# A selective scan in a four-layer decoder: the products with B move from TensorE to GpSimd

## The reference

```python
def _mamba_forward(x, ln_g, ln_b, W_in, conv_w, conv_b, W_x, W_dt, dt_bias, A_log, D, W_out):
    L = x.shape[1]
    xn = _layer_norm(x, ln_g, ln_b)
    xz = jnp.einsum('ble,de->bld', xn, W_in)
    u, z = (xz[..., :DIN], xz[..., DIN:])
    up = jnp.pad(u, ((0, 0), (DCONV - 1, 0), (0, 0)))
    uc = sum((conv_w[:, k] * up[:, k:k + L, :] for k in range(DCONV))) + conv_b
    u = jax.nn.silu(uc)
    dbc = jnp.einsum('bld,rd->blr', u, W_x)
    dt_in = dbc[..., :DTR]
    Bm = dbc[..., DTR:DTR + DSTATE]
    Cm = dbc[..., DTR + DSTATE:]
    dt = jax.nn.softplus(jnp.einsum('blr,dr->bld', dt_in, W_dt) + dt_bias)
    dA = jnp.exp(dt[..., None] * -jnp.exp(A_log))
    dBu = dt[..., None] * Bm[:, :, None, :] * u[..., None]

    def step(h, e):
        da, dbu, c = e
        h = da * h + dbu
        y = jnp.einsum('bdn,bn->bd', h, c)
        return (h, y)
    ...
    _, ys = jax.lax.scan(step, h0, elems)
    y = (jnp.moveaxis(ys, 0, 1) + u * D) * jax.nn.silu(z)
    return x + jnp.einsum('bld,ed->ble', y, W_out)
```

## Time and profile before

| quantity | value |
|---|---|
| median of 3 runs | 1628.07 us (1625.56 to 1632.83) |
| profiled execution | 1626.36 us |
| its span | 1624.5 us |
| mean granted clock of PE | 0.961 of full speed |
| busy, whole span | PE 1413.6, DVE 953.5, ACT 685.6, POOL 348.1 us |
| first and last start of a scan | 554.0 and 754.2 us |
| 554.0 to 600.8 us | PE busy 44.8, DVE 26.4, ACT 23.5, POOL 13.0 us |

### The profile page before, as it was taken

The page is one execution under the profiler, slowest core; times in us unless marked ns, Lnnn a source line. Parts: engine busy times, 40 slices in busy tenths (PEclk is TensorE's granted clock), DMA queues, the critical chain, the costliest instruction groups (busy, mean ns, idle before and its releaser), DMA issues.

```text
span 1624.5 us, 25636 instructions
## 1 busy us (share of the span) xinstructions
PE 1413.6 (87%) x9708; PEld 918.2 (57%) x9708; DVE 953.5 (59%) x2240; ACT 685.6 (42%) x1932; POOL 348.1 (21%) x293
## 2 busy tenths in 40 slices
PE   7999776888787999998887638989998999989997
PEld 4666543555555566665554425555566666656664
DVE  2556567666654455566767786655675455653334
ACT  4555324565554544342454203632234555422222
POOL 1333004433431232131500034200100333410000
PEclk9999989999998999999998979999999999999999
DMA  9000000000000400000000000000000000000000
GB/s 375 1 1 1 1 1 1 1 1 1 1 1 14 196 1 1 0 1 1 1 2 1 0 1 1 2 1 0 0 2 2 1 1 1 1 1 1 0 0 13
DMA packets 4225, 25.72 MB, mean 16 GB/s; under 512 B 1168, under 2 KB 3216, under 8 KB 3472
## 3 DMA queue, kind: packets, MB, share of 16 engines
q1 hardware_dynamic: 4112, 24.19, 3.7%
HBM read 23.67 MB, written 0.52 MB: 15 GB/s over the span
## 4 chain that ended last, share of the span: by engine, by line
PE 72%; DVE 15%; ACT 6%; issue 4%; POOL 1%; DMA 1%; DVEq 0%; SPq 0%; ACTq 0%; POOLq 0%
PE PS L1071 6%; PE PS L641 5%; PE PS L1056 4%; PE PS L1057 4%; PE PS L325 4%; PE PS L1912 4%; PE PS L357 3%; PE PS L1890 3%; PE PS L337 3%; PE PS L707 3%; PE PS L1903 2%; PE PS L298 2%; PE PS L306 2%; PE PS L366 2%; PE PS L319 2%
## 5 line engine op out<-in xcount | busy, mean ns | idle before, releaser
L549 POOL TENSOR_TENSOR arena<-arena,small 128x768 f32<-128x768 f32 (+1 forms) x64 | 107.8, 1684 | 225.7 <-DVE small L492 116.8
L877 DVE TENSOR_REDUCE arena<-PS 128x2 f32<-128x512 f32 (+1 forms) x192 | 108.8, 609 | 53.5 <-PE PS L635 52.4
L804 ACT ACTIVATE arena<-PS 128x512 f32<-128x512 f32 (+1 forms) x192 | 92.2, 532 | 107.2 <-PE PS L641 107.2
L2104 DVE TENSOR_TENSOR_SCAN arena<-arena,PS 128x512 f32<-128x512 f32 x64 | 78.1, 1220 | 81.3 <-PE PS L1890 70.3
L1160 DVE TENSOR_TENSOR arena<-arena,PS 128x512 f32<-128x512 f32 x82 | 56.4, 688 | 117.1 <-ACT arena L1093 117.0
L1093 ACT ACTIVATE arena<-PS 128x512 f32<-128x512 f32 x82 | 49.0, 597 | 167.9 <-PE PS L1057 167.9
L429 ACT ACTIVATE arena<-PS,small 128x256 f32<-128x256 f32 (+1 forms) x256 | 110.8, 453 | 0.0
L641 PE MATMUL PS<-arena 32*128 32x256 f32 (+1 forms) x768 | 97.7, 371 | 13.8 <-DVE arena L877 9.5
L635 PE MATMUL PS<-arena 32*128 32x256 f32 (+1 forms) x768 | 94.7, 372 | 2.2 <-DVE arena L877 1.6
L500 DVE COPY arena<-PS 128x768 f32<-128x768 f32 (+1 forms) x64 | 69.5, 1086 | 34.6 <-PE PS L337 34.6
L641 PEld LDWEIGHTS PS<-arena 32*128 32x128 f32 x768 | 64.0, 185 | 42.3 <-ACT arena L804 30.4
...
## 6 DMA issues: line engine op xcount, KB each, us to landing
...
w_rest<-in_rest SPq DMA_DIRECT2D x1, 6493.5 KB, 38.3
...
```

The costliest lines, as they stand in the source:

```text
L549: g.tensor_tensor(p, p, ri, ALU.mult).then_inc(self.pn_done.sem, 1)
L804: a.activation(self.PT[:, q % 8, :], PS[:, 3 + q % 3, 0:2 * n], ACT.Exp).then_inc(self.e_done.sem, 1)
L877: v.tensor_reduce(dst, src, AX.X, ALU.max, negate=True).then_inc(self.mx_done.sem, 1)
```

## The change

The products dt*u*B are no longer matmuls. For each step PE spreads the row of B over the partitions like that of C (`spread_b`), up to five steps ahead, into bank 5; ACT copies it to one of four SBUF buffers (`b_copy`); GpSimd multiplies it with dt*u (`product`) into one of four SBUF buffers `dB`; and the scan reads decays and products, both from SBUF. The transposes, the diagonals and the copy `turned` are gone.

Both spreads are now bf16 matmuls. So that no precision is lost, B and C are computed three times, on partitions 0, 32 and 64, and `parts` on GpSimd turns them into three bf16 parts (a value rounded to bf16, what is left rounded, and what is left then), which one matmul over 96 partitions adds up. The row of C has one bank (4) in place of two, the sum over the states one (6) in place of two; B's spread and the output projection share bank 5. The next batch's `inputs` are cut into four pieces of two matmuls (n = 0 to 3) and `gates` (n = 4); ACT's silus, selections and logarithms come one step later each; `gate` comes at n = 1 and `finish` at n = 4. The decays keep four buffers, at another place of the arena.

```diff
@@ Mamba.__init__
-        self.dc_done, self.dc_ev, self.bt_ev = s("dc_done", B, 1), s("dc_ev", B, 1), s("bt_ev", B, 1)
+        self.dc_done, self.dc_ev = s("dc_done", B, 1), s("dc_ev", B, 1)
+        self.part_step = s("part_step", 7 * B, 1)
-        self.tr_done, self.tr_ev = s("tr_done", B, 1), s("tr_ev", B, 1)
-        self.diag_ready = s("diag_ready", G // 4, 1)
-        self.da_ready, self.db_done, self.c_done = s("da_ready", G, 1), s("db_done", G, 1), s("c_done", G, 1)
+        self.b_done, self.bs_ready, self.db_ready = s("b_done", G, 1), s("bs_ready", G, 1), s("db_ready", G, 1)
+        self.da_ready, self.c_done = s("da_ready", G, 1), s("c_done", G, 1)
...
-        self.CB, self.BT = t(4108, 2, 256), t(4620, 2, 32)
-        self.ab, self.rl, self.lw, self.ex = t(4684, 512), t(5196, 512), t(5708, 512), t(6220, 512)
-        self.dt, self.dtu = t(6732, 2, 512), t(7756, 512)
-        self.dtuT = t(8268, 2, 2, 256)
-        self.diag = t(9292, 24, P)
-        self.dA = t(12364, 4, 512)
-        self.h, self.hC = t(14412, 2, 512), t(15436, 3, 512)
-        self.y = t(16972, 512)
+        self.DBC, self.BC = t(4108, 2, 256), t(4620, 256).bitcast(BF16).rearrange("p (b s) -> p b s", b=2)
+        self.rest = t(4876, 256)
+        self.ab, self.rl, self.lw, self.ex = t(5132, 512), t(5644, 512), t(6156, 512), t(6668, 512)
+        self.dt, self.dtu = t(7180, 2, 512), t(8204, 512)
+        self.bs, self.dB = t(8716, 4, 256), t(9740, 4, 512)
+        self.h, self.hC = t(11788, 2, 512), t(12812, 3, 512)
+        self.y = t(14348, 512)
         self.r = t(0, 512)
+        self.dA = t(14860, 4, 512)
@@ tensor
...
+            for k in taps:
+                ins = pe.matmul(PS[:, self.bank(b, part), part * 256:part * 256 + 256],
+                                self.WK[:, k, part * P:(part + 1) * P], self.XNT[:, b, k:k + 256],
+                                start=(k == 0), stop=(k == 3), skip_group_check=True)
+            if taps[-1] == 3:
+                ins.then_inc(self.uz_done.sem, 1)
...
-            for t in range(2):
-                for j in range(2):
-                    ins = pe.matmul(PS[:, 0, 256 + t * 16:272 + t * 16], u[:, j * 256 + t * P:j * 256 + t * P + P],
-                                    self.wB[:, j, :], start=(j == 0), stop=(j == 1), skip_group_check=True)
...
-        def turn(b):
-            pe.wait_ge(self.chain_step.sem, self.chain_step.at(0, 5 * b + 5))
-            pe.wait_ge(self.bt_ev.sem, self.bt_ev.at(0, b + 1))
-            for t in range(2):
-                for j in range(2):
-                    ins = pe.transpose(PS[:, 0, t * 256 + j * P:t * 256 + j * P + P],
-                                       self.dtu[:, j * 256 + t * P:j * 256 + t * P + P], c.ident)
-            ins.then_inc(self.tr_done.sem, 1)
-
-        def drive(g):
+        def spread_b(g):
             b, n = divmod(g, self.N)
             if n == 0:
-                pe.wait_ge(self.tr_ev.sem, self.tr_ev.at(0, b + 1))
-            if n % 4 == 0:
-                pe.wait_ge(self.diag_ready.sem, self.diag_ready.at(0, g // 4 + 1))
+                pe.wait_ge(self.part_step.sem, self.part_step.at(0, 7 * b + 7))
             if g == 0:
-                pe.wait_ge(self.xn_ev.sem, self.xn_ev.at(0, 1))
-            elif g == 1:
                 pe.wait_ge(self.xn_ev.sem, self.xn_ev.at(0, 2))
             else:
-                pe.wait_ge(self.sc_ready.sem, self.sc_ready.at(0, g - 1))
-            for t in range(2):
-                for j in range(2):
-                    ins = pe.matmul(PS[:, 2 + g % 2, j * 256 + t * P:j * 256 + t * P + P],
-                                    self.dtuT[:, b % 2, t, j * P:(j + 1) * P], self.diag[:, g % 12 * 2 + t, :],
-                                    start=True, stop=True, skip_group_check=True)
-            ins.then_inc(self.db_done.sem, 1)
-
-        def spread(g):
+                pe.wait_ge(self.bs_ready.sem, self.bs_ready.at(0, g))
+            if b and n == 9:
+                pe.wait_ge(self.z_ready.sem, self.z_ready.at(b - 1, 1))
+            pe.matmul(PS[:, 5, 0:256], self.onehot[0:96, n:n + 1].to_broadcast([96, P]),
+                      self.BC[0:96, b % 2, :], start=True, stop=True).then_inc(self.b_done.sem, 1)
...
+
+        def spread_c(g):
             b, n = divmod(g, self.N)
+            if n == 0:
+                pe.wait_ge(self.part_step.sem, self.part_step.at(0, 7 * b + 7))
             if g == 0:
                 pe.wait_ge(self.xn_ev.sem, self.xn_ev.at(0, 3))
-            if n == 0:
-                pe.wait_ge(self.dc_ev.sem, self.dc_ev.at(0, b + 1))
-            if g >= 2:
-                pe.wait_ge(self.hc_ready.sem, self.hc_ready.at(0, g - 1))
-            pe.matmul(PS[:, 4 + g % 2, 0:256], self.onehot[32:48, n:n + 1].to_broadcast([16, P]),
-                      self.CB[32:48, b % 2, :], start=True, stop=True).then_inc(self.c_done.sem, 1)
+            else:
+                pe.wait_ge(self.hc_ready.sem, self.hc_ready.at(0, g))
+            pe.matmul(PS[:, 4, 0:256], self.onehot[0:96, 16 + n:17 + n].to_broadcast([96, P]),
+                      self.BC[0:96, b % 2, :], start=True, stop=True).then_inc(self.c_done.sem, 1)
...
+            if b and n == 0:
+                pe.wait_ge(self.y_ready.sem, self.y_ready.at(0, b))
...
+            g = min(self.N * (b + 1) + 9, self.G)
+            pe.wait_ge(self.bs_ready.sem, self.bs_ready.at(0, g))
...
-        keep_warm(c, pe, 5, 36)
-        turn(0)
-        drive(0)
-        spread(0)
+        keep_warm(c, pe, 3, 16)
+        for g in range(5):
+            spread_b(g)
         for i in range(self.G):
             b, n = divmod(i, self.N)
-            if i + 1 < self.G:
-                drive(i + 1)
-                spread(i + 1)
-            if i >= 2:
-                add(i - 2)
-            if b and n == 4:
+            spread_c(i)
+            if i:
+                add(i - 1)
+            if i + 5 < self.G:
+                spread_b(i + 5)
+            if b and n == 3:
                 outputs(b - 1)
             if b + 1 < B:
-                if n < 3:
-                    inputs(b + 1, n)
-                if n == 6:
+                if n < 4:
+                    inputs(b + 1, n // 2, (0, 1) if n % 2 == 0 else (2, 3))
+                if n == 4:
+                    gates(b + 1)
@@ scalar
...
-            a.activation(self.CB[0:48, b % 2, :], PS[0:48, 0, 0:256], ACT.Copy).then_inc(self.dc_ev.sem, 1)
-            a.activation(self.BT[:, b % 2, :], PS[:, 0, 256:288], ACT.Copy).then_inc(self.bt_ev.sem, 1)
+            a.activation(self.DBC[0:104, b % 2, :], PS[0:104, 0, 0:256], ACT.Copy).then_inc(self.dc_ev.sem, 1)
...
+        def b_copy(g):
+            a.wait_ge(self.b_done.sem, self.b_done.at(0, g + 1))
+            if g >= 4:
+                a.wait_ge(self.db_ready.sem, self.db_ready.at(0, g - 3))
+            a.activation(self.bs[:, g % 4, :], PS[:, 5, 0:256], ACT.Copy).then_inc(self.bs_ready.sem, 1)
...
+        b_copy(0)
+        b_copy(1)
         for g in range(self.G):
             b, n = divmod(g, self.N)
-            if g == 0:
-                decays(0)
-                turned(0)
-            else:
-                decays(g)
-            if n == 1 and b:
-                turned(b)
+            decays(g)
+            if g + 2 < self.G:
+                b_copy(g + 2)
@@ parts (new), chain (its five instructions now issued one by one)
+    def parts(self, eng, b):
+        step, full, BC, r = 7 * b, self.DBC[:, b % 2, :], self.BC[:, b % 2, :], self.rest
+
+        def after(ins, k):
+            ins.then_inc(self.part_step.sem, 1)
+            eng.wait_ge(self.part_step.sem, self.part_step.at(0, step + k))
+
+        eng.wait_ge(self.dc_ev.sem, self.dc_ev.at(0, b + 1))
+        after(eng.tensor_copy(BC[0:96], full[0:96]), 1)
+        for k in (1, 2):
+            s = slice(32 * k, 32 * k + 32)
+            after(eng.tensor_tensor(r[s], full[s], BC[s], ALU.subtract), 2 * k)
+            after(eng.tensor_copy(BC[s], r[s]), 2 * k + 1)
+        after(eng.tensor_tensor(r[64:96], r[64:96], BC[64:96], ALU.subtract), 6)
+        after(eng.tensor_copy(BC[64:96], r[64:96]), 7)
@@ vector
...
-            v.wait_ge(self.db_done.sem, self.db_done.at(0, g + 1))
+            v.wait_ge(self.db_ready.sem, self.db_ready.at(0, g + 1))
             if g >= 2:
                 v.wait_ge(self.hc_ready.sem, self.hc_ready.at(0, g - 1))
-            v.tensor_tensor_scan(self.h[:, g % 2, :], self.dA[:, g % 4, :], PS[:, 2 + g % 2, :], 0.0,
+            v.tensor_tensor_scan(self.h[:, g % 2, :], self.decay(g), self.dB[:, g % 4, :], 0.0,
...
-            if b and n == 3:
+            if b and n == 1:
                 gate(b - 1)
-            if b and n == 5:
+            if b and n == 4:
                 finish(b - 1)
@@ gpsimd
...
-                ins = g.tensor_tensor(self.diag[:, at:at + 8, :].rearrange("p (n t) k -> p n t k", t=2)[:, :, t, :],
-                                      c.ident.unsqueeze(1).to_broadcast([P, 4, P]),
```

(34 more changed lines are left out.)

155 lines of the change are left out of this document (69 added, 86 removed).

## The result

The changed kernel takes 1616.07 us (median of 6 runs, 1613.27 to 1618.54) against 1627.74 before; the ratio is 0.9926, with a 95% interval of 0.9907 to 0.9944. It is 0.74% faster. The forecast was 1631.8, no difference; the measured time lies in its range, and the sign is the other one. The profiled execution took 1613.27 us, its span is 1611.5.

A forecast was written before the change was run, and what follows sets the result against it. PE's products were taken to bound the scan; afterwards, turns between scan and GpSimd product. Steps, boundaries and extras saved 16.3 us, the clock cost 20.0: +3.7, so 1631.8 us; range 1609 to 1651, the forecast's own 1622 to 1642.

The forecast's parts named there:

- 63 steady steps: Mid-batch scan starts: 2.23 us apart, a scan's turn of 1.09 plus a GpSimd product's turn of 1.14.
- three boundaries over the steady step: Change from one batch to the next: GpSimd's splits and time-step chain add 12.8 us each, 38.4 for three.
- TensorE's clock: PE falls to 1.2 GHz at the start and in each boundary, costing 15.0 us behind boundaries and 5.0 in the last batch.
- all else in the stage: DVE's gate, last tile's sum, statistics and scaling, and PE's output matmuls waiting for the spare bank: together 5 us.
- What bounds the kernel: In the scan stage, the scan on DVE waited 70.3 us for PE's products with B, which the change removes.
- Turns: Scan on DVE and product on GpSimd, both reading SBUF, exclude each other: a step of 2.23 us, not 1.93.
- The boundary: Listed GpSimd's splits, chain and products and DVE's scans from end of scan 9 through scan 16: 28.4 us against 15.6.
- 2.0 a step: Cost of half clock in the next batch's first steps, where PE also has inputs; 2.5 steps, 5.0 us, three times.
- two: Rival for the whole kernel: scan and product take turns but the clock stays; 1612 us, chance 0.20.
- One: Rival for the whole kernel: the scan takes no turn, step 1.93 us; 21 us saved, 1607, chance 0.10.
- Three: Rival: the clock falls and does not return while the stage lasts, since PE waits each step; 1648 us, chance 0.26.
- Unknown prices: Instructions without a profile row: bf16 spread on PE 0.27 us, ACT's copy of B 0.38, GpSimd's product 1.27.

## Why the prediction was wrong

The forecast for the span of the scans was 200.2 + 3.7 = 203.9 us; it is 184.8. By its own steps:

| term | forecast | measured |
|---|---|---|
| 63 steady steps | 2.23 each, 140.5 | 2.15 each, 135.5 |
| three boundaries over the steady step | 38.4 | 30.7 |
| TensorE's clock | 20.0 | 5.0 |
| all else in the stage (measured: what the other rows leave) | 5 | 13.6 |
| sum | 203.9 | 184.8 |

**What bounds the kernel:** right. PE's products went, and with them the wait of 70.3 us; scans now wait 13.1 us for GpSimd's products.

**Turns:** right, and it is why the change brings so little. A scan behind a whole instruction of GpSimd ends 1.08 after it, where 1.09 was forecast. The product's own part of the turn is 2.15 - 1.08 = 1.07 and not 1.14: the product overlaps with the scan by 0.2 and not by 0.13. The step is 0.08 shorter than forecast; times 63, 5 us.

**The boundary:** the list of events was right, the sum too long. From the end of scan 9 to the end of scan 16 (575.41 + 1.44 to 602.12) the trace has 25.3 us (25.3 at the other two boundaries as well), the forecast 28.4. The casts took 0.39 and the differences 0.66, where 0.56 and 0.73 were taken, and the forecast let scans and GpSimd follow one another also where they overlapped. That the logarithms would be hidden behind the splits was not quite right: splits and decays came at the same time (585.0 and 585.28), and without the splits scan 12 waited for ACT as long as before. That the steps behind it are GpSimd's is shown: without the splits 11.5 us of the stage go, with the chain on DVE 14.5.

**The clock is the step that failed.** It fell where the forecast said, and it also came back as forecast, where PE was busy without a gap: PE worked 3.50 of the 3.50 us from 603.0 to 606.5 at 0.50, and the clock was 0.97 from 606.5 to 610.5. The price was wrong, and it is the term that was mis-sized: 20.0 forecast, 5.0 measured with the clock held up. "2.0 a step" for 2.5 steps, three times, counts PE's lateness as DVE's. But behind a boundary GpSimd had the chain and a backlog of products, DVE had the gate, and steps took 2.7 to 2.9 us without PE. At half clock PE has 2.7 a step (1.92 for the sum, 0.4 for each spread), so it was late for nobody. Behind each of the first two boundaries only one step met inputs at 1.2 GHz (1.91 at 604.93, 1.74 at 653.06), not two and a half. Piece by piece: the first steps of the three sequences with inputs were to cost 5.0 each and cost 1.7, 1.1 and 0.7; the last sequence was to cost 5.0 and cost 1.4. In the whole stage DVE's output products waited 2.2 us for the row of C, 1.6 of it at 563.40. Held at this size the forecast would have read 1631.8 - 15 = 1616.8; that it then meets the 1616.07 is in part luck, since the other terms were off by 5, 8 and 9 us in both directions and the 3.0 us behind the stage had no term.

**All else:** 5 was too little. The closing DVE instruction of a batch waits for PE, 5.4 us in four times, of which 4.2 in three lie ahead of the last scan:

```profile
DVE Z L2126 <- PE PS L1910: 5.4, 4, 1.9
```

The forecast had 0.8 for it. ACT's silus cost the scan a wait of 1.0 (at 573.48 above) in each of three sequences and had no price in the sum. The step with the gate should have cost 0.3; the scan behind it ends 3.4 us after the one before (604.27 to 607.63, the starts plus the durations), 1.2 over 2.15, since it loses its place in the turn. With the statistics and the scaling of the last batch, 3.5 us where 3 were taken (the steps at 717.73 and 732.38 are 1.8 and 1.7 over 2.15), an estimate from these rows is 14 us, about the 13.6 that are left over.

**The rivals:** two (turns, clock without a price, 1612) was the nearest, 4 us off, at 0.20. One fell with the first scan of 1.44. Three had the clock fall and stay low. It came back in each sequence, the last one included (1.00 from 706 to 722), and stayed at 0.50 only from 722.8 to 736.5. That the fall would be cheap was in the forecast's own words ("it costs nothing, GpSimd is late there") and should have been carried on into the following steps.

**Unknown prices:** the bf16 spread took 0.27 (taken: 0.27), the copy of B 0.36 to 0.38 (0.38), the product 1.26 alone (1.27). The range held the time; the chances had 0.38 on no difference and 0.27 on faster.
